# An attention and gated-FFN layer on one core: the shift rows are moved to the front of SyncE's step, the denominators are compacted one step later, and the widened reciprocals get a second buffer

## What is computed

```python
# _L0_attn_ref
Q = _split_heads(x, H)                 # the queries are x itself
K = _split_heads(x @ Wk + bk, H)
V = _split_heads(x @ Wv + bv, H)
scores = jnp.einsum('bhqd,bhkd->bhqk', Q, K) + mask      # causal mask
attn = jax.nn.softmax(scores, axis=-1)
o = jnp.einsum('bhqk,bhkd->bhqd', attn, V).transpose(0, 2, 1, 3).reshape(B, S, -1)
return x + jax.nn.gelu(o, approximate=False) @ Wf + bf
# _L0_ffn_ref
h = jax.nn.silu(x @ wg.T) * (x @ wu.T)
return h @ wd.T
# reference
x = _layernorm(x + _L0_attn_ref(x, ...))
x = _layernorm(x + _L0_ffn_ref(x, ...))
```

## Time and profile before

| | |
|---|---|
| median of 3 runs | 2197.97 us (2195.44 to 2216.67) |
| the profiled execution's own time | 2213.07 us |
| its span, first to last instruction | 2211.1 us |
| busy, share of the span | PE 88%, DVE 68%, POOL 51%, ACT 47% |
| granted TensorE clock, mean | 0.928 of full speed |
| attention loop | about 80 to 1640 us |
| feed-forward loop | about 1652 us to the end |

### The profile page before, as it was taken

One profiled execution on the slowest core, in us unless ns is written; L12 is line 12 of the kernel. 1 busy time (PEld: TensorE's weight loads), 2 busy tenths in 40 slices (PEclk: granted clock), 3 DMA queues, 4 the chain that ended last, 5 costly groups with the idle time before them and its releaser, 6 DMA issues. The chain is left out here.

```text
span 2211.1 us, 38994 instructions
## 1 busy us (share of the span) xinstructions
PE 1935.3 (88%) x10304; PEld 999.6 (45%) x10304; DVE 1496.8 (68%) x3598; ACT 1044.7 (47%) x1523; POOL 1128.5 (51%) x1192
## 2 busy tenths in 40 slices
PE   5799988988997898999888999977879889999996
PEld 4344434444443343444333344322336667666664
DVE  3786767767685776767676767765736767767764
ACT  1155444544554454454445545533544545545543
POOL 0186666666676666665666676664751212212212
PEclk9699999999999999999999999887989999999998
DMA  8434334343433434343343434362126465575530
GB/s 285 152 129 153 135 128 163 111 146 128 154 132 122 163 115 149 120 161 134 121 158 120 150 120 156 111 193 98 66 59 152 136 179 130 155 179 133 163 105 20
DMA packets 257657, 303.12 MB, mean 137 GB/s; under 512 B 24736, under 2 KB 174368, under 8 KB 257584
## 3 DMA queue, kind: packets, MB, share of 16 engines
q1 hardware_dynamic: 257584, 302.24, 43.0%
HBM read 174.20 MB, written 127.93 MB: 137 GB/s over the span
## 5 line engine op out<-in xcount | busy, mean ns | idle before, releaser
L930 ACT ACTIVATE weights<-ring 128x1024 f32<-128x1024 f32 (+3 forms) x768 | 601.4, 809 | 498.9 <-PE ring L677 488.8
L647 POOL TENSOR_TENSOR weight_sum<-weight_sum,weights 128x512 f32<-128x512 f32 (+3 forms) x448 | 681.9, 1522 | 9.6
L677 PE MATMUL o_acc<-weights,v_pair 128*64 128x512 f32 (+3 forms) x3072 | 647.6, 531 | 12.5 <-POOL weights L625 9.7
L677 PE MATMUL ring<-q_stack,k_stack 50*128 50x512 f32 (+3 forms) x1536 | 322.6, 425 | 163.1 <-DMA q_stack<-shifts 117.9
L625 POOL TENSOR_SCALAR_AFFINE_SELECT weights<-weights 128x256 f32<-128x256 f32 x512 | 219.2, 431 | 417.6 <-ACT weights L930 414.7
L1080 DVE TENSOR_REDUCE part_max<-ring 128x2 f32<-128x1024 f32 x256 | 303.6, 1207 | 137.7 <-PE ring L677 137.5
L1088 DVE CUSTOM_DVE_ANT_0 scrap<-ring,causal 128x128 bf16<-128x128 f32 (+3 forms) x512 | 230.6, 488 | 232.8 <-PE ring L677 231.2
L668 POOL TENSOR_TENSOR h_lo<-hidden,h_hi 128x512 f16<-128x512 f32 x96 | 114.5, 1194 | 446.1 <-ACT h_hi L898 446.1
L677 PE MATMUL ring<-k_stack,q_stack 48*128 48x512 f32 (+3 forms) x1536 | 317.1, 416 | 25.8 <-DMA k_stack<-k_rows 16.7
L677 PEld LDWEIGHTS ring<-q_stack,k_stack 50*128 50x128 f32 x1536 | 153.8, 197 | 380.5 <-issue 128.9
L677 PEld LDWEIGHTS o_acc<-weights,v_pair 128*64 128x64 f32 x3072 | 180.7, 143 | 252.6 <-issue 222.2
(11 more groups left out here) (105 smaller groups left out, 2199.7 us busy)
## 6 DMA issues: line engine op xcount, KB each, us to landing
v_pairs<-v_unit SPq DMA_DIRECT2D x64, 512.0 KB, 4.9
v_pair<-v_pairs SPq DMA_DIRECT2D x64, 512.0 KB, 4.4
o_heads<-o_pair SPq DMA_DIRECT2D x64, 512.0 KB, 5.4
g<-o_heads SPq DMA_DIRECT2D x16, 2048.0 KB, 19.3
den_wide<-reciprocals SPq DMA_DIRECT2D x32, 1024.0 KB, 13.0
q_stack<-q_rows SPq DMA_DIRECT2D x128, 192.0 KB
k_stack<-k_rows SPq DMA_DIRECT2D x128, 192.0 KB
q_rows<-x_hi SPq DMA_DIRECT2D x32, 512.0 KB, 5.5
```

The source lines that it names most:

```text
L647: pool.tensor_tensor(dst, other, W[t][:, :, :], ALU.add).then_inc(s_add, 1)
L677: return nc.tensor.matmul(o, l, r, start=start, stop=stop)
L930: nc.scalar.activation(W[t][:, :, :], bank_of("t", t)[:, :, 0:width_of(t)], ACT.Exp).then_inc(s_w, 1)
```

## The change

In SP's step, `move_shifts` and `load_shifts` come first and `load_stacks` after them. On DVE, `shift_turn` follows `shift_lo` directly, where a row-maximum instruction of the next tile stood between them. `load_den` moves from steps with k = 2 to steps with k = 3, ahead of store_o and store_den; the reciprocals move from burst 2 of a k = 3 step to burst 5 of the next k = 0 step, and their store from k = 3 to k = 1; the attention loop gets one more (empty) step for them, and the last `store_rec` follows the loop. `den_wide` gets a second buffer, which lies over the q_stack buffers, so its first load (unit 1) waits until the last transposed scores are made. The wait of `load_dn` becomes that for the norm two units back. In `finish`, `load_g` now stands ahead of `load_dn`. The norm of unit 0 moves from behind step 65 into steps 60 to 63, two slices a step.

```diff
@@ SP, the attention step
+                if 1 <= r <= PAIRS:
+                    move_shifts(n - 1)
+                    load_shifts(r - 1, n - 1)
                 if r + 1 < PAIRS:
                     load_stacks(r + 1, it)
-                if 1 <= r <= PAIRS:
-                    move_shifts(r - 1, n - 1)
-                if 1 <= r <= PAIRS:
-                    load_shifts(r - 1, n - 1)
...
+                if r % 4 == 3 and 7 <= r < 4 * GROUPS + 7:
+                    load_den((r - 7) // 4 + it)
                 if 3 <= r < PAIRS + 3:
                     store_o(r - 3, n - 3)
                     store_den(r - 3, n - 3)
-                if r % 4 == 2 and 6 <= r < 4 * GROUPS + 6:
-                    load_den((r - 6) // 4 + it)
-                if r % 4 == 3 and 7 <= r < 4 * GROUPS + 7:
-                    store_rec((r - 7) // 4 + it)
+                if r % 4 == 1 and 9 <= r < 4 * GROUPS + 9:
+                    store_rec((r - 9) // 4 + it)
...
-                if r == PAIRS + 1:
+                if r == PAIRS + LEAD:
+
+                    sp.wait_ge(s_st, NS * PAIRS)
                     load_dn(1, 0)
@@ SP, load_dn
-                if r >= 1:
-
-                    sp.wait_ge(s_gn, HC * n)
+                if r >= 2:
+
+                    sp.wait_ge(s_gn, HC * (n - 1))
@@ SP, the feed-forward step
                 if r + 2 < UNITS:
+                    load_g(r + 2, it)
+                if r + 2 < UNITS:
                     load_dn(r + 2, it)
-                if r + 2 < UNITS:
-                    load_g(r + 2, it)
@@ DVE, the attention step
                         if what == "s" and j == 0 and 1 <= r <= PAIRS:
                             shift_lo(r - 1, n - 1)
-                        if what == "s" and j == 1 and 1 <= r <= PAIRS:
                             shift_turn(r - 1, n - 1)
+                    if b == 6 and PAIRS - 4 <= r < PAIRS:
+                        norm(0, 0, range(2 * (r - PAIRS + 4), 2 * (r - PAIRS + 5)))
...
-                    if b == 2 and k == 3 and 7 <= r < 4 * GROUPS + 7:
-                        reciprocals((r - 7) // 4 + it, r == 7)
-                if r == PAIRS + 1:
-                    norm(0, 0, range(HC))
-
+                    if b == 5 and k == 0 and 8 <= r < 4 * GROUPS + 8:
+                        reciprocals((r - 8) // 4 + it, r == 8)
```

More of the change, by code:

```diff
@@ L149, in build @@
         xn = [sb(f"xn{i}", [P, UT, D], F32) for i in range(2)]
-        dn = sb("den_wide", [P, HC, U], F32)
+        dn0 = sb("den_wide0", [P, HC, U], F32)
         wf_sb = sb("wf_sb", [P, HC, D], F32)
@@ L157, in build @@
         RING = 4
-        Q = [sb(f"q_stack{i}", [HSTEP + SROWS + SHROWS, S], F32R) for i in range(RING)]
+        qctx = ExitStack()
+        Q = [sb(f"q_stack{i}", [HSTEP + SROWS + SHROWS, S], F32R, qctx) for i in range(RING)]
+        qctx.close()
+        dn = [dn0, sb("den_wide1", [P, HC, U], F32)]
         K = [sb(f"k_stack{i}", [HSTEP + SROWS + SHROWS, S], F32R) for i in range(RING)]
@@ L224, in build @@
         s_wrest = sem("ffn_weights_ready")
-        s_passed = {e: sem(f"passed_{e}") for e in ("sp", "pool", "pe", "dve")}
+        s_passed = {e: sem(f"passed_{e}") for e in ("sp", "act", "pool", "dve")}
         s_xt = sem("xt_loaded")
@@ L262, in build @@
         s_xn = [sem(f"xn_loaded{i}") for i in range(2)]
-        s_dn = sem("den_wide_loaded")
+        s_dn = [sem(f"den_wide_loaded{i}") for i in range(2)]
         s_gn = sem("g_normalised")
@@ L347, in added @@
             return sum(i <= t for i in ADDS)
-        STEPS_B = PAIRS + 4
-        LOOP_B = (STEPS_B, 8, 4, UNITS - ALONE - 3)
+        STEPS_B = PAIRS + 5
+        LOOP_B = (STEPS_B, 12, 4, UNITS - ALONE - 4)
         STEPS_C = UNITS + 1
@@ L432, in store_o, with move_shifts @@
                              osb[r % 2][:]).then_inc(s_ost[r % 2], 16)
-            def move_shifts(r, n):
+            def move_shifts(n):
                 sp.wait_ge(s_shs, n + 1)
@@ L439, in move_shifts @@
                     sp.dma_start(sd[bass.ds(n, 1)].rearrange("o h m (u s q) -> (o h m u) s q", s=P // SQ, q=SQ)[:, i],
-                                 shiftT[SQ * i:SQ * (i + 1), :].bitcast(F32)).then_inc(s_shd, 16)
+                                  shiftT[SQ * i:SQ * (i + 1), :].bitcast(F32)).then_inc(s_shd, 16)
             def load_shifts(r, n):
@@ L448, in load_shifts @@
                     sp.dma_start(Q[r % RING][row:row + SHROWS, :].bitcast(F32),
-                                 sd[bass.ds(n, 1), h].rearrange("o m t -> (o m) t")).then_inc(s_shl[r % RING], 16)
+                                  sd[bass.ds(n, 1), h].rearrange("o m t -> (o m) t")).then_inc(s_shl[r % RING], 16)
             def store_den(r, n):
@@ L539, in load_dn @@
                 n = r + 2 * it
-                if r >= 1:
-                    sp.wait_ge(s_gn, HC * n)
+                if r >= 2:
+                    sp.wait_ge(s_gn, HC * (n - 1))
                     settle(sp, s_passed["sp"])
                 for h in range(2):
-                    sp.dma_start(dn[DV * h:DV * (h + 1)], rd[bass.ds(b, 1), h:H:2, t0:t0 + U].rearrange(
-                        "o c t -> (o c) t").partition_broadcast(DV)).then_inc(s_dn, 16)
+                    sp.dma_start(dn[r % 2][DV * h:DV * (h + 1)], rd[bass.ds(b, 1), h:H:2, t0:t0 + U].rearrange(
+                        "o c t -> (o c) t").partition_broadcast(DV)).then_inc(s_dn[r % 2], 16)
             load_x(0, True)
@@ L575, in _ @@
             walk(sp, *LOOP_B, attend)
+            store_rec(GROUPS - 1)
             for i in range(2):
@@ L1140, in norm @@
                     if c == 0:
-                        dve.wait_ge(s_dn, 32 * (n + 1))
+                        dve.wait_ge(s_dn[r % 2], 32 * (r // 2 + it + 1))
                         dve.wait_ge(s_g[r % 2], 16 * (r // 2 + it + 1))
-                    v.tensor_tensor(g[r % 2][:, c], g[r % 2][:, c], dn[:, c], ALU.mult).then_inc(s_gn, 1)
+                    v.tensor_tensor(g[r % 2][:, c], g[r % 2][:, c], dn[r % 2][:, c], ALU.mult).then_inc(s_gn, 1)
             def attend(r, it):
```

## The result

| | before | changed |
|---|---|---|
| median | 2198.84 us, 20 runs (2190.01 to 2216.67) | 2218.57 us, 20 runs (2209.42 to 2230.48) |
| the profiled execution: its own time, its span | 2213.07, 2211.1 us | 2221.82, 2220.1 us |
| ratio to before | 1 | 1.0084, 95% interval 1.0066 to 1.0102 |

The change makes the kernel slower by 0.84%, about 20 us. That is less than the 1% that the prediction took as about the least that a measurement can tell from none, but with 20 runs of each kernel the interval lies wholly above 1. The prediction was 2104 us, 4.3% faster, with a range of 2030 to 2176: it was wrong in sign. The profiled execution of before lies 14 us above its median and that of the changed kernel only 3 above its own, so the two traces differ by 9.0 us of the medians' 19.7. A stretch by stretch comparison accounts for those 9.

A forecast was written before the change was run, and what follows sets the result against it. It took PE's work, clock and idle waits for shifts as the bound, in the feed-forward loop a ring through one queue. -98 - 60 - 8 + 45 + 4 - 5 + 3 + 25 = -94 from 2197.97 gave 2104 us, range 2030 to 2176.

The forecast's parts named there:

- All 29 waits go: -98: Attention loop up to step 57: PE's 29 waits for q_stack<-shifts all vanish, -98 us.
- the clock: -60: Attention loop: without idle times of 3 to 5 us PE's clock returns to 1.00, -60 us, bounds -76 and -30.
- Stack loads behind the shifts: +45: Attention loop: stacks, issued after the shifts, land 3.2 us late once in four steps, +45 us, bounds 0 and +135.
- The upper bound, +135 by 10.4 us a group: Stack loads' worst case: k = 2 and 3 also slip 1 to 2 us, each late step loses 1.7 us of clock.
- The Trainium skill's rule: Stack loads: 2.0 us fixed plus bytes over 436 GB/s, so 3.8 us, never late, and their term 0.
- the queue becomes the ring: Rival, chance 0.07: in the attention loop, leftover stores stretch the ring from stacks through maxima to next stacks; slower, 2285 us.
- ready some 1.8 us into the step: Attention steps: estimated time at which the transposed maxima are ready for the shift store.
- Steps 58 to 60: -5: Attention loop's end: PE waits for the stacks near 15 us where it was 20, -5 us, bounds -15 and +10.
- Norm slices: +3: Norm of unit 0 moved: +6 us in steps 60 to 63, -3.5 behind step 65, net +3.
- Reciprocals: -8: Attention loop: 24.8 us of DVE idle in 11 waits go, a third counted, -8 us, bounds 0 and -25.
- The feed-forward loop: +25: Last loop: the norm waits for g, xn and den_wide, 1.8 us in each of 14 units, +25, bounds 0 and +55.

The follow-up runs named there:

- the order alone: The kernel before with only SP's order changed, move_shifts and load_shifts ahead of load_stacks: 2306.49 us, ratio 1.0473.
- The kernel with only the old order: The changed kernel with SP's old order again, stacks first and then the shifts, all else of the change kept: 2172.38 us, ratio 0.9875.

## Why the prediction was wrong

The 52 steps can now be added up from measured kernels. Taking all waits away gives 1105.0 - 1259.4 = -154. The rest of the change in these steps costs 1117.5 - 1105.0 = +12.5, which is the early transpose. The late stacks of the changed kernel cost 1237.2 - 1117.5 = +120. The sum is -22, as measured. The prediction had -98 - 60 - 8 = -166 and +45. This is one way to divide the time: what the earlier transpose and the new place of the denominators give while stacks are late is inside the +120.

**"All 29 waits go: -98" and "the clock: -60"** were right as the worth of the waits that go: 154 against 158. In the changed kernel the missing clock did not come back, 66.6 us of 71.7, since new waits took the place of the old. PE waits for the shifts once, near step 59, and SP waits 2.2 us for their store, not 9.2. The reading of the earlier trace rows, a small store behind a load on three engines, held: with that load spread, the old order needs no change.

**"Stack loads behind the shifts: +45"** is the step that failed: it is +120. The new waits alone are 83.8 us, where it forecast 13 times 3.2, 42. Its mechanism and its timetable held almost to the microsecond in step 33, a k = 1 step: shifts landed at +7.6 (forecast +8), stacks issued at +8.7 (+8.7), PE 3.71 us late in step 34 (3.2). Three sizes were wrong.

- The stacks take 14.4 us from first issue to use, where I took 13 from bounds of 12.4 and 15.2. The waits at the start of k = 2 steps are 55.2/13 = 4.2 us.
- The stacks were to be issued at +5.4 in the other steps. They are issued at +7.7 in k = 3 steps, +8.8 in k = 0 and +13.8 in k = 2 (medians; +9.3 in k = 1). The k = 2 and 0 steps, some 28 us long here, mostly leave room for that. But the k = 3 steps also end late, which I called even. In step 31, which begins at 787.6, the shift store is issued at 789.91, as expected, but 4.0 us pass until its load, not 2.8. The stacks are issued at +7.6 and not +5.4, and PE, which needs them after 20 us, waits 2.06. The empty-queue price of the earlier trace rows does not hold with stores queued.
- The clock that these waits cost. I added 0.3 us a group of four for it. All in all a group takes 1237.2/13 = 95.2 us and 1117.5/13 = 86.0 with the loads spread: 9.2 a group. The waits are 6.4 of it. The missing clock is 66.6 us and not 1.7, 5.0 a group, so that the rest goes to the clock, though some missing clock must lie where PE was not the bound.

```profile
789.91 1.88 SPq L442 DMA_DIRECT2D shifts<-shiftT  x4
793.95 0.71 SPq L451 DMA_DIRECT2D q_stack<-shifts  x2
795.23 1.76 SPq L411 DMA_DIRECT2D q_stack<-q_rows  x2
```

The upper bound, +135 by 10.4 us a group, was sound; the value was not. It called three of four kinds of step "even" by a margin of 2.6 us, which came from an average step and an empty queue; it needed the length and the queue of each kind. And the sum took back 60 us of clock for the old waits while it charged next to nothing for the new ones.

**The Trainium skill's rule** ("DMA: Bandwidth & Descriptors", the anatomy of one DMA), which would have made the stacks take 3.8 us, does not hold for the loads as they are: 14.4 us at 78 GB/s. The section gives it for DMAs that GpSimd issues, and these are issued by SyncE. For one 16-row load of 64 KB it gives 2.0 + 0.15 = 2.15 us, an estimate by that page of the Trainium skill, and the trace agrees:

```profile
q_stack<-q_rows SPq DMA_DIRECT2D x384, 64.0 KB, 2.2
```

The twelve of a step take longer, since SP needs 6.3 us to issue them.

**The rival "the queue becomes the ring"** was the true mechanism for the order alone. That its 2285 lies near the measured 2306 is in part luck: it had +62 in the steps and +25 in the last loop, and the kernel with the order alone has +76 in the 52 steps and none in the last loop, which it leaves as it was. In the order-only kernel and in the changed one the early transpose cuts the loss by 58 to 68 us, which the prediction used without counting: "ready some 1.8 us into the step" holds for k = 1 and 3 (1.5 and 1.9). At k = 0 and 2 the transpose comes at +3.4 and +3.5 even when no stack is late, and in the changed kernel at +4.0 and +6.8 (medians; up to +8.5 at k = 2), because a row maximum before it needs scores, and these the late stacks. I gave this rival 0.07, because the bytes behind the stacks "drain within the step". Before, SP waited out the landing of the shifts, 9.2 us, between the stacks and these bytes, and by then the stacks were through; v_pair and v_pairs now land in 12.3 and 12.5 us instead of 4.4 and 4.9.

**Steps 58 to 60: -5.** Measured +8.4. The wait for PE was forecast "near 15 where it was 20": it is 7.2 for the rows of pair 58 and 12.3 for the stacks behind them, 19.5 in all, and 5.5 more for the stacks of step 58: 24.9 where it was 20.0. The shift store of step 59 is issued at 1460.25, behind the batch, and its load at 1477.70:

```profile
1460.25 2.61 SPq L442 DMA_DIRECT2D shifts<-shiftT  x4
1477.70 0.55 SPq L451 DMA_DIRECT2D q_stack<-shifts  x2
```

```profile
1492.76 0.47 PE L682 MATMUL ring<-k_stack,q_stack 48*128 48x128 f32 x2 [12.29 <-DMA k_stack<-k_rows]
```

The bound of +10 held. The first two norm slices, in step 60, also fall into this stretch.

**Norm slices: +3.** Measured +13 by the medians of the kernel that puts them back; in its trace 7.1 us of that lie in steps 61 to 63 and up to 4.4 in step 60, and 0.4 in the stretch behind. Two slices took 3.44 us in one step, where I set 2.9 at most, and they stand ahead of a row maximum that PE waits for, so the "5 us free" of DVE did not cover them. POOL pays there too, as forecast, with additions of 2.78 to 2.84 us that take 2.37 without; but DVE pays more, 2.83 us for the second slice. The gain of 3.5 behind step 65 did not show. That stretch is 4.0 us longer, but it is still 3.6 us longer with the norm put back, and 68.2 to 69.0 us in the three kernels of the experiments that leave the denominators where they were, so the norm is not the cause. The wait for den_compact in it is 29.5 us instead of 17.1 mainly because the 11.4 us of the norm no longer lie in front of it.

**Reciprocals: -8.** The 11 waits went, as said, but the size was wrong, outside its bounds of 0 and -25. In the new order with the early transpose, the new place of the denominators is worth 1273.2 - 1237.2 = 36 us in the 52 steps. The prediction counted DVE's waits only; SP's 72.4 us of waiting for their store go too, and I take these for the reason, since in that order what holds SP holds up the next stacks. With spread loads it is worth nothing (1104.6 against 1105.0). The kernel with only the old order has 52 steps that are 50 us shorter than before; how these divide between the denominators and the earlier transpose was not tried apart.

**The feed-forward loop: +25.** Measured +5, and even that is not sure: five kernels of the experiments have the same feed-forward code and take 538.9 to 543.5 us, and three have that of before and take 538.9 to 543.9. It was right that the second buffer brings nothing while its load stands behind load_g, and the wait moved to den_wide, 46.9 us in 14 where it was 46.2 for g. But g lands in 8.3 us without den_wide ahead of it, and the norm's slices wait for den_wide alone, so the 2.1 us a unit that I set for xn and the later start did not come.

The order of the parts' sizes is thus: the stack term 75 us off, the early transpose, which had no cost in the sum, and the reciprocals together 20 off (+12.5 for -8), steps 58 to 60 13 off, the norm and the end of the loop 9 off (+7.8 and +4.0 for +3), and the feed-forward loop 20 off the other way, which hid part of the miss. That the medians lie 19.7 us apart and the traces 9.0 comes from the execution of before that was profiled, 14 us above its median; what made it longer was not looked for.

## What to carry to other kernels

Before a transfer is moved ahead of a slow one, look at why the slow one is slow: a share of 0.19 during a load says how few engines it keeps busy, and cutting that load to spread it was worth 168 us where every reordering around it was worth less. A wait that is removed by order is only gone if what now stands second has slack in the shortest step of the period, with the queue as it is there; work out each kind of step, and price the clock together with the waits that remain. A second buffer helps only if its load is issued ahead of the instruction that blocks the queue: here that was 53 us.

## What the runs showed of the hardware

- A load that keeps about three of sixteen DMA engines busy, by its share of 0.19, holds up everything that is issued right behind it: a 512 KB transfer took 12.5 us instead of 4.9 to land, and the issuing of one store took SP 6.31 us. In steps 6 to 57 of the changed kernel 51 DMAs took SP over 4 us to issue; with the same slow loads and the wait for the shift store between, none did. Three times as many transfers of a third the size took 2.3 us more of issuing and ended that.
- 29 waits of 2.9 us on average in 1237 us went with a mean clock of 0.95; with none it was 1.00 over 1105 us.
- A multiplication of two SBUF tiles of 128x512 on DVE took 0.69 us alone and 2.83 us beside additions of 2.78 to 2.84 us on POOL, in each of steps 60 to 63 of the changed kernel.
- The same edit, the early transpose, saved 58 to 68 us with the stack loads late and cost about 13 with none late.
